# Routed expert tiles with features on partitions, gate-and-up weights copied to a fixed place, and early gathers paced by the shared expert

## The reference

```python
logits = einsum('btc,ec->bte', x, router_w)            # 16 experts
top_vals, top_idx = top_k(logits, 2); gates = sigmoid(top_vals)
gate, up = split(einsum('nc,ech->neh', xf, gate_up_w)) # 256 -> 2 x 256, for each expert
h = silu(gate) * up
out_all = einsum('neh,ehc->nec', h, down_w)            # 256 -> 256
moe = sum over the two chosen experts of gates * out_all
shared = (silu(x @ shared_gate.T) * (x @ shared_up.T)) @ shared_down.T   # hidden size 512
return x + moe + shared
```

## Time and profile before

| what | value |
|---|---|
| median of three timed runs | 1411.06 us |
| lowest and highest of them | 1407.27 and 1411.35 us |
| span of the profiled execution, first to last instruction | 1379.5 us |
| PE busy in that span | 1255.7 us (91%) |
| POOL busy | 523.9 us (38%) |
| granted TensorE clock, mean | 0.977 of full |

### The profile page before, as it was taken

One profiled execution on the slowest core, in us unless ns is written; L12 is line 12 of the kernel. 1 busy time (PEld: TensorE's weight loads), 2 busy tenths in 40 slices (PEclk: granted clock), 3 DMA queues, 4 the chain that ended last, 5 costly groups with the idle time before them and its releaser, 6 DMA issues. The chain is left out here.

```text
span 1379.5 us, 18247 instructions
## 1 busy us (share of the span) xinstructions
PE 1255.7 (91%) x5694; PEld 569.1 (41%) x5694; DVE 888.8 (64%) x2045; ACT 663.2 (48%) x1243; POOL 523.9 (38%) x731
## 2 busy tenths in 40 slices
PE   6898989989999999999999999998899888999996
PEld 3232433323343224453453444443242334666663
DVE  5889789788877986458557567568768423233332
ACT  2355455566555655556546556446656551012221
POOL 4444251163312411326217227225423122456665
PEclk9799999999999999999999999999999999999998
DMA  8472513324330333033123123124622004934341
GB/s 262 131 245 81 159 49 96 109 65 147 110 106 24 108 93 108 22 87 108 47 63 108 47 62 108 47 62 123 139 85 48 17 16 118 337 99 55 55 54 16
DMA packets 113216, 131.53 MB, mean 95 GB/s; under 512 B 17017, under 2 KB 93305, under 8 KB 112867
## 3 DMA queue, kind: packets, MB, share of 16 engines
q1 hardware_dynamic: 102867, 119.91, 30.0%
q0 software_dynamic: 10256, 10.45, 4.6%
HBM read 83.25 MB, written 48.40 MB: 95 GB/s over the span
## 5 line engine op out<-in xcount | busy, mean ns | idle before, releaser
L1288 DVE TENSOR_REDUCE Mx<-bank 128x1 f32<-128x512 f32 x512 | 339.0, 685 | 206.6 <-PE bank L1022 204.5
L904 ACT ACTIVATE prob<-bank 128x512 f32<-128x512 f32 x576 | 332.4, 594 | 257.2 <-PE bank L1048 255.6
L1048 PE MATMUL bank<-QS,KS 99*128 99x512 bf16 x768 | 296.1, 387 | 40.1 <-ACT prob L904 19.5
L1022 PE MATMUL bank<-KS,QS 96*128 96x512 bf16 x768 | 296.9, 388 | 14.2 <-DVE Mx L1285 8.0
L1061 PE MATMUL bank<-prob,V 128*17 128x512 f32 x1536 | 206.6, 610 | 0.7 <-ACT prob L904 0.7
L904 ACT ACTIVATE prob<-prob 128x512 f32<-128x512 f32 x192 | 120.9, 629 | 159.4 <-DVE prob L1299 158.5
L1048 PEld LDWEIGHTS bank<-QS,KS 99*128 99x128 bf16 x768 | 74.8, 98 | 234.2 <-ACT prob L904 130.3
L1022 PEld LDWEIGHTS bank<-KS,QS 96*128 96x128 bf16 x768 | 76.0, 99 | 123.0 <-issue 47.2
L1285 DVE CUSTOM_DVE_ANT_0 bank<-bank,ff_h 128x512 f32<-128x512 f32 x128 | 87.9, 696 | 20.6 <-PE bank L1022 20.0
L741 POOL TENSOR_SCALAR parts<-rest 128x512 bf16<-128x512 f32 x47 | 29.1, 620 | 183.4 <-DVE rest L1248 182.8
L727 POOL TENSOR_SCALAR shift<-mv 128x4 f32<-128x4 f32 x28 | 5.5, 197 | 233.5 <-DVE mv L1209 233.5
(11 more groups left out here) (180 smaller groups left out, 1833.2 us busy)
## 6 DMA issues: line engine op xcount, KB each, us to landing
stack_scr<-parts SPq DMA_DIRECT2D x48, 384.0 KB, 2.6
QS<-stack_scr SPq DMA_DIRECT2D x47, 384.0 KB, 4.1
KS<-stack_scr SPq DMA_DIRECT2D x47, 384.0 KB, 5.0
stack_scr<-parts SPq DMA_DIRECT2D x48, 256.0 KB, 2.9
w_gu<-in_gate_up SPq DMA_DIRECT2D x16, 512.0 KB, 9.6
stack_scr<-parts SPq DMA_DIRECT2D x48, 128.0 KB, 2.9
cT<-in_ctxT SPq DMA_DIRECT2D x8, 512.0 KB, 5.8
w_dn<-in_down SPq DMA_DIRECT2D x16, 256.0 KB, 10.0
```

The costliest lines, as they stand in the source:

```text
L904: act.activation(prob[:, u % NP_, j, :], src, ACT.Exp, scale=CAST).then_inc(exp_done, 1)
L1022: pe.matmul(m, QS[0:STACK, h, qt * P:(qt + 1) * P], KS[0:STACK, h, :], start=True, stop=True).then_inc(s_full, 1)
L1048: pe.matmul(bankT[e % NT][:, :], KS[0:ROWS, h, kt * P:(kt + 1) * P], QS[0:ROWS, h, :], start=not on_pe, stop=True).then_inc(t_full, 1)
L1288: dve.tensor_reduce(dst, b, AX.X, ALU.max).then_inc(s_read, 1)
```

## The change

Per routed tile, the roles of the two operands in the gate-and-up product are exchanged. The weights become the stationary operand, in eight blocks of 128x128 (four blocks of features times two of the contraction), and xT, 128 columns, streams; the result has features on partitions, which is what the down product wants. turn_hidden and the copy to hTt go. Since the stationary operand would otherwise have an address out of a register, ACT copies the tile's 128x1024 gate-and-up weights to a fixed place (stage, into w_now, two buffers, which lie over the second half of hid), one tile or two ahead. The down products get four PSUM banks in place of two, and each comes one tile earlier in PE's program (behind the gate-and-up product of the next tile and no longer of the one after that). NX is 28, and the early gathers 8 to 11, 13, 15, 17 and 20 to 23 each wait for a step of the shared expert (after_sum: DVE's adds, after_gate: ACT's silus).

```diff
-        NX = 30
+        NX = 28
...
+        w_now = hid[:, 1, :, :].rearrange("p (i k) n -> p i k n", i=2)
...
-        ht = sb("ht", [P, 2, EH], F32)
-        hTt = sb("hTt", [P, 2, EH // P, P], F32)
+        ht = sb("ht", [P, 2, EH // P, P], F32)
...
+        n_last = (LATE - 1) * QT
+        after_sum = {8 + i: n_last - QT + 1 + i for i in range(QT)}
+        after_gate = {13 + 2 * i: LATE * HT - HT + 2 + i for i in range(HT - 1)}
+        after_sum.update({20 + i: n_last + 1 + i for i in range(QT)})
...
                 for s in range(NX):
+                    if s in after_sum:
+                        pool.wait_ge(y_read, after_sum[s])
+                    if s in after_gate:
+                        pool.wait_ge(sg_done, after_gate[s])
                     rows(s)
...
-                for s in range(TILES + 2):
+
+                def stage(s):
+                    e = act.value_load(tile_expert[0:1, s:s + 1], min_val=0, max_val=NE - 1)
+                    act.activation(w_now[:, s % 2, :, :].rearrange("p k n -> p (k n)"),
+                                   w_gu[:, bass.ds(e, 1), :, :].rearrange("p a k n -> p (a k n)"),
+                                   ACT.Identity).then_inc(staged, 1)
+
+                act.wait_ge(w_in, 32 * NE)
+                act.wait_ge(y_full, (LATE - 1) * QT)
+                stage(0)
+                stage(1)
+                for s in range(TILES + 1):
                     if s < TILES:
...
                         act.activation(sgt[:, s % 2, :], bank[2 + s % 2][:, 0:EH], ACT.Silu).then_inc(sg_ready, 1)
-                    if s >= 2:
-                        n = s - 2
+                    if s + 2 < TILES:
+                        stage(s + 2)
+                    if s >= 1:
+                        n = s - 1
                         act.wait_ge(yt_full, n + 1)
                         if n >= NY:
                             act.wait_ge(sum_out[n % NY], 16 * (n // NY))
-                        act.activation(yt[:, n % NY, :], bank[6 + n % 2][:, 0:D], ACT.Identity,
+                        act.activation(yt[:, n % NY, :], bank[4 + n % 4][:, 0:D], ACT.Identity,
...
-                def turn_hidden(s):
...
-                def gate_up_product(s, e):
+                def gate_up_product(s):
                     pe.wait_ge(xT_read, s + 1)
+                    pe.wait_ge(staged, s + 1)
                     if s >= 2:
                         pe.wait_ge(h_ready, s - 1)
-                    for k in range(KD):
-                        ins = pe.matmul(bank[2 + s % 2][:, :], xT[:, s % 3, k, :],
-                                        w_gu[:, bass.ds(e, 1), k, :].rearrange("p a n -> p (a n)"),
-                                        start=(k == 0), stop=(k == KD - 1))
+                    for m in range(2 * EH // P):
+                        for k in range(KD):
+                            ins = pe.matmul(bank[2 + s % 2][:, m * P:(m + 1) * P],
+                                            w_now[:, s % 2, k, m * P:(m + 1) * P],
+                                            xT[:, s % 3, k, :], start=(k == 0), stop=(k == KD - 1))
                     ins.then_inc(gu_full, 1)
 
                 def down_product(s, e):
-                    pe.wait_ge(hT_read, s + 1)
-                    if s >= 2:
-                        pe.wait_ge(yt_read, s - 1)
+                    pe.wait_ge(h_ready, s + 1)
+                    if s >= 4:
+                        pe.wait_ge(yt_read, s - 3)
...
-                    dve.wait_ge(hT_full, s + 1)
-                    if s >= 2:
-                        dve.wait_ge(yt_full, s - 1)
-                    dve.tensor_copy(hTt[:, s % 2, :, :].rearrange("p k n -> p (k n)"),
-                                    bank[4 + s % 2][:, 0:EH]).then_inc(hT_read, 1)
```

More of the change, by code:

```diff
@@ L1508, in experts @@
         gu_full = sem("gu_full")
+        staged = sem("staged")
         sg_ready = sem("sg_ready")
         h_ready = sem("h_ready")
[L1511 to L1512 removed]
         yt_full = sem("yt_full")
@@ L1656, in turn_rows @@
                     ins.then_inc(xT_full, 1)
-                def turn_hidden(s):
-                    pe.wait_ge(h_ready, s + 1)
-                    if s >= 2:
[L1661 to L1665, removed]
-                def gate_up_product(s, e):
+                def gate_up_product(s):
                     pe.wait_ge(xT_read, s + 1)
+                    pe.wait_ge(staged, s + 1)
                     if s >= 2:
                         pe.wait_ge(h_ready, s - 1)
-                    for k in range(KD):
-                        ins = pe.matmul(bank[2 + s % 2][:, :], xT[:, s % 3, k, :],
-                                        w_gu[:, bass.ds(e, 1), k, :].rearrange("p a n -> p (a n)"),
-                                        start=(k == 0), stop=(k == KD - 1))
+                    for m in range(2 * EH // P):
[3 more added lines that the diff above has]
+                                            xT[:, s % 3, k, :], start=(k == 0), stop=(k == KD - 1))
                     ins.then_inc(gu_full, 1)
                 def down_product(s, e):
-                    pe.wait_ge(hT_read, s + 1)
-                    if s >= 2:
-                        pe.wait_ge(yt_read, s - 1)
+                    pe.wait_ge(h_ready, s + 1)
+                    if s >= 4:
+                        pe.wait_ge(yt_read, s - 3)
                     for k in range(EH // P):
-                        ins = pe.matmul(bank[6 + s % 2][:, 0:D], hTt[:, s % 2, k, :],
+                        ins = pe.matmul(bank[4 + s % 4][:, 0:D], ht[:, s % 2, k, :],
                                         w_dn[:, bass.ds(e, 1), k, :].rearrange("p a n -> p (a n)"),
@@ L1692, in _ @@
                 expert = []
-                for s in range(TILES + 2):
+                for s in range(TILES + 1):
                     if s < TILES:
                         expert.append(pe.value_load(tile_expert[0:1, s:s + 1], min_val=0, max_val=NE - 1))
-                        gate_up_product(s, expert[s])
+                        gate_up_product(s)
                     if s + 2 < TILES:
@@ L1700, in _ @@
                         pe.wait_ge(y_read, LATE * QT)
[L1701 to L1704, removed]
+                    if s >= 1:
+                        down_product(s - 1, expert[s - 1])
             @block.vector
```

7 lines of the change are left out of this document (3 added, 4 removed).

## The result

| | median us | lowest to highest, runs |
|---|---|---|
| before | 1410.20 | 1407.27 to 1411.35, 4 |
| changed | 1392.45 | 1389.35 to 1392.92, 4 |

The ratio is 0.9867 (0.9846 to 0.9888): 18 us faster. The forecast was 1411.5 us and no change, with a range of 1406.5 to 1417.

What follows compares the result with a forecast made beforehand. It took POOL's chain of scatters, with landings and SP, as the bound: span 1379.5 - 0.9 (earlier scatter 0) + 1.3 (late gather) = 1379.9, plus 31.6 to the median gives 1411.5 us, range 1406.5 to 1417.

Steps and rivals of the forecast that it cites:

- the 31.6 us between this span and the median: Last term of the sum: added unchanged to the forecast span of 1379.9 us to give 1411.5 us.
- The other early gathers: Gathers beside the shared expert: PE waits for none of them, pacing uses up POOL's idle time ahead of scatter 0; zero.
- The bound: Routed tiles: from the first scatter on, POOL's scatters, their landings and SP bound the kernel; PE is held back.
- PE's tile: PE per routed tile: 2.95 us for 3.01, with the gate-and-up product at 1.87 us; lower bound 2.79 per tile.
- ACT: ACT per routed tile: weight copy 1.03 us and register reading 0.45 added, 2.33 us in all, hidden behind the scatters.
- Scatter 0: Start of POOL's scatters: at 1230.4, 0.9 us earlier, behind gathers 23 to 27; yt of tile 0 done about 1229.3.
- The last store: Ahead of scatter 0: lands at 1226.7, 3.4 us after DVE's last add, with 3.7 us of cover.
- The late gathers: Two more gathers among the scatters: behind scatter 34 costs nothing, behind scatter 36 adds 1.3 us.
- The rivals: Alternatives: PE bound (7%), weight loads not hidden (7%), ACT bound (6%), landings of scatters change (6%).
- PE is the bound: Rival, routed tiles: PE bounds and its tiles get shorter, 3 to 10 us less, around 1403 us; 7%.

Runs made afterwards that it cites:

- e10: Kernel before with only the waits of the early gathers added (30 early gathers, old tiles): 1390.35 us, before beside it 1410.79, ratio 0.9842.
- e11: Kernel before, unchanged, run again for its trace: 1410.21 us, before beside it 1410.79, ratio 0.9997.
- e5: Kernel before with 39 routed tiles for 47, the last eight left out: 1364.95 us, before beside it 1383.40, ratio 0.9877.
- e6: Changed kernel with 39 routed tiles, the last eight left out: 1366.10 us, kernel before beside it 1383.40, ratio 0.9882.
- e3: Changed kernel, run again as it is: 1381.69 us, kernel before beside it 1381.16, ratio 1.0000.
- e1: Changed kernel without the waits of its early gathers (new tiles only, NX 28): 1381.70 us, kernel before beside it 1381.37, ratio 1.0005.
- e15: Changed kernel with a memset behind each of the attention part's 24 tag scatters: 1382.93 us, kernel before beside it 1380.88, ratio 1.0013.
- e17: Changed kernel with a memset behind each of the 24 tag scatters, as e15, once more: 1382.30 us, kernel before beside it 1381.54, ratio 1.0000.
- e14: Kernel before with the early gathers' waits and a memset behind each of the 24 tag scatters: 1384.91 us, before beside it 1411.24, ratio 0.9798.
- e2: Kernel before with only the waits of the early gathers added, same kernel as e10: 1380.61 us, before beside it 1381.37, ratio 0.9996.
- e7: Kernel before with the gate-and-up product made half as long again by repeated multiplications: 1449.17 us, before beside it 1411.52, ratio 1.0272.
- e9: Changed kernel without the waits of its early gathers, same kernel as e1: 1407.99 us, kernel before beside it 1410.79, ratio 0.9974.
- e12: Kernel before with 24 early gathers for 30, still in a row, the others behind scatters: 1412.34 us, before beside it 1411.24, ratio 1.0006.
- e13: Kernel before with 24 early gathers and a memset behind each: 1395.82 us, before beside it 1411.24, ratio 0.9878.
- e0: Kernel before, unchanged, run again for its trace: 1379.97 us, before beside it 1381.37, ratio 0.9986.

## Why the prediction was wrong

**The step that failed** is in the sum: "with the 31.6 us between this span and the median". I took it for "start, end and the difference between two executions". With start and end at 1.7 us, nearly 30 us were left that the trace in hand could not show, and I carried them over as a constant. They were work of the long occasion that the change removes in part. The second failure hangs on it: "The other early gathers ... Zero". The edit was costed on a trace in which the gathers hold up nobody. On the long occasion 28 to 30 gathers in a row hold up the shared expert, and spacing them takes 22 to 24 us off the way to scatter 0: 74.7 for 96.9 us in e10 and e11, of one group, and 73.0 in the changed kernel, where the chain is 140.7 for 140.5 and the end 7.5 for 7.5. The attention part, the same in both, ended later, with the experts' part beginning at 1170.0 for 1164.6; kernels with this attention part lie between 1160.8 and 1170.0 on long occasions, and why is not shown. The sum is -18.3, against spans of 1391.2 and 1409.5.

**What held, by the prediction's steps.**
- *The bound.* The scatters, from the first on; e5 and e6 show it in both kernels, and on the quick occasion e3 ended where the forecast had it: a span of 1381.5 for 1379.9. That is closer than the terms: against the trace of before, with its experts' part from 1157.3 us on and its scatters as in the earlier trace rows, that part began 1.9 us later, the way to scatter 0 was 2.3 shorter and the chain 2.5 longer, where 0, -0.9 and +1.3 were forecast.
- *PE's tile.* 2.86 for 2.95 us. The pair of load and stream takes 0.111 us, not 0.117, nearer to the lower bound of 0.107; the product 1.78 for 1.87. The Trainium skill (TensorE: Matmul & The Clock Gate, Part 3, What overlaps and what doesn't) has a load overlap a matmul in flight only where their row groups differ. The 16 loads of all 128 rows beside 16 streams of 128 columns in 1.78 us disagree with it; in turn they would have taken 3.58 by the prediction's rows.
- *ACT.* The copy 1.06 for 1.03 us. Reading the expert's number leaves ACT idle 0.25 us, not 0.45.
- *Scatter 0.* In e3 it came at 1230.94, forecast 1230.4, and for the forecast's reason: gathers 23 to 27 stand ahead of it, and yt of tile 0 was done at 1229.86, forecast 1229.3. The size is partly luck: DVE's last add ended at 1224.45, 1.2 us later than reckoned, and gather 23 started 0.26 us behind it and not 0.94. In the profile of the result POOL waited 1.13 us for yt instead: PE's down product ended at 1239.30 and ACT was free at 1239.94, but ACT started only at 1241.60, a small rest of the hold-up. The last store was covered.
- *The late gathers.* 1363.80 to 1366.98 is 3.18 us, as forecast. But the 36 steps up to there took 120.80 us against 122.05, so the chain grew by 0.1 and not 1.3. In e3 it grew by 2.5: those 36 steps took 123.2 us, two of them 1.6 and 0.9 us longer than before (19 to 20, and 34 to 35), for which no run shows a cause. In e1, e15 and e17 it is 140.5 to 140.7.
- *The rivals.* "PE is the bound" named a faster time, around 1403, for a wrong reason. None of the rivals was the true one: a burst on POOL that holds up the other engines.

**What stays open.** Why an occasion is quick or long: the chip alone does not decide it, and no trace shows what differs. Where the posts are held: the trace shows waits that end late and not on which path. The Trainium skill (DMA: Bandwidth & Descriptors, SWDGE vs HWDGE vs iDMA) has GpSimd's software write every descriptor of such a transfer into rings in SBUF; a burst is then a stretch of dense writing by GpSimd, but no run here shows that this is what the posts wait behind. All these executions were timed together with a recorded span and clock, so they don't tell whether the recording takes part. About 4 us of the long occasion are left in e14.

## What to carry to other kernels

Set the profiled execution's own time beside the timed ones before anything else: here a difference of 30 us was work that the trace did not show, not a constant to carry over. A row of indirect transfers issued by GpSimd one behind the other is not free because nobody waits for its data; spread it out, by other work or by waits for steps that are under way anyway, and look for engines whose waits end "remote" while it runs. Shortening engines that stand off the bound gave nothing here (e1, e3), and an edit that only spaced transfers gave 1.6% on a long occasion and nothing on a quick one (e10, e2).

## What the runs showed of the hardware

- On some occasions, indirect transfers issued every 1.25 us by GpSimd delay engines that wait for another engine's semaphore: from about ten gathers in, some 26 us for VectorE's last add, until 4.4 to 5.2 us behind the end of the last gather (e7, e9, e11, e12; 30, 28, 30 and 24 in the row). With a memset of 0.54 us between them, 1.66 us apart, 24 of them delayed none (e13). On quick occasions 30 in a row delay none (e0).
- Eight in a row come with a small delay on a long occasion: with the 24 tag scatters 0.4 us further apart, an add waits 3.99 us instead of 6.60, and the time is 5.4 us less (e14, e10; two groups).
- TensorE's granted clock was 0.50 from 1222 to 1238 us in e11, while it stood idle from 1217.05 to 1238.31 in the hold-up.
- Such an occasion holds for all runs of a group: before took 1410.2, 1411.5, 1410.8 and 1411.2 on four long ones, 1381.4, 1381.2, 1383.4, 1380.9 and 1381.5 on five quick ones.
- Full 128x128 float32 weight loads every 0.111 us beside streams of 128 columns: 16 of each in 1.78 us (the changed kernel).
